# A two-layer transformer kernel: layer 0's opening in another order, and the stacked rows loaded in eight outer steps

## The reference, cut to what matters

```python
# layer 0: x is 8 x 512 x 128; c is 8 x 128
mod = (silu(c) @ wmod).reshape(8, 6, 1, 128)         # sa, ca, ga, sb, cb, gb; ga, gb kept >= 0.25 in size
h = layernorm(x) * (1 + ca) + sa
x = x + ga * attention0(h)
x = x + gb * top1_experts(layernorm(x) * (1 + cb) + sb)

def attention0(h):                                   # 16 heads of 8, 64 landmarks
    q_l, k_l = means of q, k over 8 neighbouring tokens
    L = softmax(q @ k_l.T); N = softmax(q_l @ k.T)
    K = softmax(q_l @ k_l.T)
    V = K.T / max(sum(K, axis=-2))
    for _ in range(6):
        KV = K @ V
        V = 0.25 * V @ (13 * I - KV @ (15 * I - KV @ (7 * I - KV)))
    return (L @ (V @ (N @ v))) @ W_proj

# layer 1, for each batch
scores = q @ k.T / sqrt(8) + bias[head, i - j]       # 16 heads, 512 tokens
bias[head, d] = sum over 21 of amp * exp(-|shp| * (d - off) ** 2)
# then a gated projection, causal attention over a latent, and 8 experts, two for each token
```

## Time and profile before

| | us |
|---|---|
| median of 3 runs (2076.03 to 2079.79) | 2079.36 |
| profiled execution, whole | 2073.5 |
| its span | 2071.5 |
| PE busy | 1779.4 (86%) |
| DVE busy | 1444.1 (70%) |
| ACT busy | 1015.6 (49%) |
| POOL busy | 857.9 (41%) |
| mean granted PE clock | 0.943 of full |

### The profile page before, as it was taken

How to read it: one execution, slowest core, us unless ns; L and a number is a source line. 1 busy time by engine, 2 the same in 40 slices (tenths; PEclk the granted TensorE clock), 3 DMA queues, 4 the chain that set the end, 5 groups by cost and what they waited for, 6 DMA issues and landing times.

```text
span 2071.5 us, 56863 instructions
## 1 busy us (share of the span) xinstructions
PE 1779.4 (86%) x21284; PEld 1306.9 (63%) x21284; DVE 1444.1 (70%) x4537; ACT 1015.6 (49%) x1992; POOL 857.9 (41%) x1253
## 2 busy tenths in 40 slices
PE   4485898898875729999999999999999999999997
PEld 2374677677763517766667666667666667766665
DVE  4574778876761127777787786787886887778765
ACT  1252544455441206666655654654654555655542
POOL 3500101110013017767655654655754663664530
PEclk7797999999996959999999999999999999999998
DMA  2512211222006411012013012012012112111211
GB/s 94 166 24 72 76 42 51 61 75 74 7 6 208 142 67 39 33 57 77 17 71 96 11 69 87 21 72 86 26 66 85 32 60 83 35 54 40 83 32 48
DMA packets 102694, 131.72 MB, mean 64 GB/s; under 512 B 14448, under 2 KB 87536, under 8 KB 101272
## 3 DMA queue, kind: packets, MB, share of 16 engines
q1 hardware_dynamic: 70600, 98.59, 14.6%
q10 hardware_dynamic: 28496, 18.10, 3.0%
q0 software_dynamic: 3328, 11.40, 1.7%
HBM read 100.05 MB, written 28.15 MB: 62 GB/s over the span
## 4 chain that ended last, share of the span: by engine, by line
PE 45%; DVE 8%; issue 6%; DMA 5%; POOL 2%; ACT 1%; ACTq 1%; SPq 1%; POOLq 0%; DVEq 0%
PE ps L1737 13%; PE ps L1752 7%; PE ps L1723 6%; PE ps L1846 5%; PE ps L1832 4%; DMA l_w_e<-in_L_ffn_w_dram 2%; DVE l_X L1900 2%; DMA l_stack<-parts_dram 2%; PE ps L1199 1%; POOL l_Y L1583 1%; PE ps L1208 1%; PE ps L1762 1%; PE ps L1783 1%; DVE l_xn L1931 1%; ACT PT L1625 1%
## 5 line engine op out<-in xcount | busy, mean ns | idle before, releaser
L1583 POOL TENSOR_SCALAR l_Y<-l_X,l_nmax 128x512 f32<-128x512 f32 (+3 forms) x1024 | 674.6, 664 | 521.1 <-PE ps L1737 286.0
L1625 ACT ACTIVATE PT<-ps 128x512 f32<-128x512 f32 (+3 forms) x1024 | 520.0, 517 | 405.8 <-PE ps L1737 356.3
L1737 PE MATMUL ps<-ident,l_Y 128*128 128x128 f32 x3328 | 549.7, 280 | 11.7 <-ACT PT L1625 7.7
L1737 PEld LDWEIGHTS ps<-ident,l_Y 128*128 128x128 f32 x3328 | 387.2, 142 | 195.3 <-issue 82.4
L1900 DVE CUSTOM_DVE_ANT_0 l_X<-ps,strips 128x512 f32<-128x512 f32 x512 | 342.1, 687 | 134.2 <-PE ps L1723 130.9
L1723 PE MATMUL ps<-l_stack 72*128 72x512 bf16 (+3 forms) x1024 | 351.0, 345 | 66.9 <-DVE l_nmax L1900 50.0
L1900 DVE CUSTOM_DVE_ANT_0 l_X<-ps,mask 128x384 f32<-128x384 f32 (+3 forms) x512 | 238.5, 485 | 41.0 <-PE ps L1723 35.6
L1752 PE MATMUL ps<-PT,v_aug 128*10 128x128 f32 x6656 | 230.1, 274 | 0.0
L1752 PEld LDWEIGHTS ps<-PT,v_aug 128*10 128x10 f32 x6656 | 156.8, 91 | 71.5 <-ACT PT L1625 42.6
L1723 PEld LDWEIGHTS ps<-l_stack 72*128 72x128 bf16 x1024 | 102.0, 100 | 102.6 <-DVE l_nmax L1900 77.3
L1832 PE MATMUL ps<-l_fT,l_w_e 128*128 128x512 f32 x256 | 138.9, 631 | 12.1 <-DMA l_w_e<-in_L_ffn_w_dram 9.3
(11 more groups left out here) (276 smaller groups left out, 2508.6 us busy)
## 6 DMA issues: line engine op xcount, KB each, us to landing
stack<-parts_dram SPq DMA_DIRECT2D x48, 384.0 KB
l_stack<-parts_dram SPq DMA_DIRECT2D x64, 288.0 KB
l_stack<-parts_dram SPq DMA_DIRECT2D x192, 96.0 KB
l_w_e<-in_L_ffn_w_dram ACTq DMA_DIRECT2D x128, 128.0 KB, 2.2
parts_dram<-l_parts SPq DMA_DIRECT2D x32, 384.0 KB, 2.5
strips<-bias_dram POOLq DMA_DIRECT2D x16, 448.0 KB, 11.2
parts_dram<-parts SPq DMA_DIRECT2D x16, 384.0 KB, 10.9
w_e<-in_L_ffn_w_dram SPq DMA_DIRECT2D x12, 256.0 KB, 5.7
```

Source lines behind the costliest of these rows:

```text
L1583: nc.gpsimd.tensor_scalar(Y[:, n % Y_BUFS, 0:w], X[:, n % X_BUFS, 0:w], -1.0, nmax[:, n % 8:n % 8 + 1], ALU.mult, ALU.add).then_inc(y_pool, 1)
L1625: nc.scalar.activation(dst, src, ACT.Exp).then_inc(moved, 1)
L1737: last = nc.tensor.transpose(ps[:, to, k * P:(k + 1) * P], Y[:, n % Y_BUFS, k * P:(k + 1) * P], ident[:])
```

## The change

- The fronts of batches 1 and 2 start at phases -8 and 1 (`front_at`) instead of -23 and -5. The others stay.
- The relative bias is computed in two halves of four slices. The exponents are VectorE's, at phases -37 and -27; ScalarE's exponentials stand at -32 and -26, GpSimd's scaling at -29 and -23, the sums at -21 and -20, and the two turns bT at -19 and -18 instead of 20 and 21.
- The halves are put together in one buffer and stored by one transfer, behind batch 0's stacks, x loads and modulation rows and before the zeros.
- The modulation is computed as columns on 128 partitions (twelve products instead of two narrow and two wide ones for each layer), worked on there, and turned once by TensorE. mods_dram and mod_row0 have their dimensions in another order.
- The marks and stacks of layer 0 come in three transfers for each of q and k, the source's outer step being the eight rows of a head and the inner one the three copies or parts (`spread`). So do those of each group in layer 1: six transfers instead of four. The order of the 72 rows changes alike for q and k.
- Waits of TensorE for w_proj, the router's weights and late constants move to where they are used.

```diff
-GAUSS_AT, REDUCE_AT, BIAS_AT, MODS_AT = -19, 2, PHASES + 2, -16
+EXPONENT_AT, SCALED_AT, REDUCE_AT, BIAS_AT, MODS_AT = (FRONT + 4, FRONT + 14), (FRONT + 12, FRONT + 18), FRONT + 20, FRONT + 22, FRONT + 10
...
+def front_at(b):
+
+    return {0: FRONT, 1: -8, 2: 1}.get(b, PHASES * b + FRONT)
...
-            [("xT", 0, FRONT + 4), ("q", 0, FRONT + 6), ("k", 0, FRONT + 6), ("v", 0, FRONT + 7)] +
+            [("xT", 0, 4), ("q", 0, 6), ("k", 0, 6), ("v", 0, 7)] +
...
+OF_CORE, OF_FRONT = ("Ks", "cs", "kT", "a0"), ("xT", "q", "k", "v")
...
+        def spread(sp, dst, dram, s, w, sem_):
+
+            for n in range(3):
+                src = [[H * w, HD], [0, 3] if s == 0 else [C * w, 3], [1, H * w]]
+                at = (3 * s + (n if s == 0 else 0)) * C * w
+                sp.dma_start(dst[3 * HD * n:3 * HD * (n + 1), s].rearrange("r h t -> r (h t)"),
+                             bass.AP(dram.tensor, at, src)).then_inc(sem_, 16)
...
-                def stack_q(b):
-
-                    sp.wait_ge(parts_stored[0], 16 * b + 16)
-                    flat = parts_dram[0].rearrange("n (d h) t -> (n d) (h t)", d=HD)
-                    for i in range(3):
-                        sp.dma_start(stack[b % 2][3 * HD * i:3 * HD * (i + 1), 0].rearrange("r h t -> r (h t)"),
-                                     flat).then_inc(stacked[0], 16)
-
-                def stack_k(b):
-
-                    sp.wait_ge(parts_stored[1], 16 * b + 16)
-                    for i in range(3):
-                        thrice = bass.AP(parts_dram.tensor, (3 + i) * C * T, [[0, 3], [H * T, HD], [1, H * T]])
-                        sp.dma_start(stack[b % 2][3 * HD * i:3 * HD * (i + 1), 1].rearrange("r h t -> r (h t)"),
-                                     thrice).then_inc(stacked[1], 16)
+                def stack_up(b, s):
+
+                    sp.wait_ge(parts_stored[s], 16 * b + 16)
+                    spread(sp, stack[b % 2], parts_dram, s, T, stacked[s])
...
+                        sp.wait_ge(bias_halves, 2)
+                        sp.dma_start(bias_dram, bias_hr).then_inc(bias_stored, 16)
...
-                    if b == 1:
-                        for k in range(2):
-                            sp.wait_ge(bias_half_ready, k + 1)
-                            sp.dma_start(bias_dram[:, k * T:(k + 1) * T], bias_hr[:]).then_inc(bias_stored, 16)
...
-                def exponent(n):
-                    if n == 0:
-                        pool.wait_ge(shp_ready, 1)
-                    gauss_chain.link(nc.gpsimd.tensor_scalar(dist[:, n % 2], off_[:], rel[:, n:n + 1], None, ALU.subtract))
-                    gauss_chain.link(nc.gpsimd.tensor_tensor(gauss[:, n], dist[:, n % 2], shp[:], ALU.mult))
-                    nc.gpsimd.tensor_tensor(gauss[:, n], gauss[:, n], dist[:, n % 2], ALU.mult).then_inc(exponent_ready, 1)
-
-                def scaled(n):
-                    pool.wait_ge(gauss_ready, n + 1)
-                    nc.gpsimd.tensor_tensor(gauss[:, n], gauss[:, n], amp[:], ALU.mult).then_inc(gauss_scaled, 1)
+                def scaled(half_):
+                    n = slice(4 * half_, 4 * half_ + 4)
+                    pool.wait_ge(gauss_ready, half_ + 1)
+                    nc.gpsimd.tensor_tensor(gauss[:, n], gauss[:, n], bc(amp[:].unsqueeze(1), [P, 4, H * KG]),
+                                            ALU.mult).then_inc(gauss_scaled, 1)
...
-                    for k in range(2):
-                        last = nc.tensor.matmul(ps[:, 0, (2 * l + k) * B:(2 * l + k + 1) * B],
+                    for k in range(6):
...
+                    if m == FRONT + 13:
+                        pe.wait_ge(mod_columns, 1)
+                        nc.tensor.transpose(ps[0:2 * 4 * B, 1, 0:P], modT[:].rearrange("p l k b -> p (l k b)"),
+                                            ident[:]).then_inc(mods_turned, 1)
...
+                def exponent(half_):
+                    part = slice(4 * half_, 4 * half_ + 4)
+                    wide_ = [P, REL // 2, H * KG]
+                    if half_ == 0:
+                        dve.wait_ge(gauss_loaded, 48)
+                        dve.wait_ge(consts_pool, 3)
+                        gauss_chain.link(nc.vector.tensor_copy(rel[:], rel_i[:]))
+                        gauss_chain.link(nc.vector.scalar_tensor_tensor(out=shp[:], in0=shp[:], scalar=-1.0, in1=shp[:],
+                                                                        op0=ALU.mult, op1=ALU.min))
+                    if half_:
+                        dve.wait_ge(exponent_ready, half_)
+                    gauss_chain.link(nc.vector.tensor_tensor(dist[:], bc(rel[:, part].unsqueeze(2), wide_),
+                                                             bc(off_[:].unsqueeze(1), wide_), ALU.subtract))
+                    gauss_chain.link(nc.vector.tensor_tensor(gauss[:, part], dist[:], bc(shp[:].unsqueeze(1), wide_), ALU.mult))
+                    nc.vector.tensor_tensor(gauss[:, part], gauss[:, part], dist[:], ALU.mult).then_inc(exponent_ready, 1)
+
+                def bias_sum(half_):
+                    part = slice(4 * half_, 4 * half_ + 4)
+                    dve.wait_ge(gauss_scaled, half_ + 1)
+                    nc.vector.tensor_reduce(bias_rel[:, part, :], gauss[:, part].rearrange("p n (h k) -> p n h k", k=KG), AX.X,
...
-                        front(b, off)
+                        front(b, m - front_at(b))
...
+                    for half_ in range(2):
+                        if m == EXPONENT_AT[half_]:
+                            exponent(half_)
+                        if m == REDUCE_AT + half_:
+                            bias_sum(half_)
...
-                    rows = [[0, 3], [H * T, 3 * HD], [1, 4 * T]]
-                    sp.dma_start(stack[0:9 * HD, 0, 4 * g:4 * (g + 1), :].rearrange("r h t -> r (h t)"),
-                                 bass.AP(parts_dram.tensor, g * 4 * T, rows)).then_inc(stacked[g], 16)
-                    for k in range(3):
-                        rows = [[0, 3], [H * T, HD], [1, 4 * T]]
-                        sp.dma_start(stack[3 * HD * k:3 * HD * (k + 1), 1, 4 * g:4 * (g + 1), :].rearrange("r h t -> r (h t)"),
-                                     bass.AP(parts_dram.tensor, (3 + k) * C * T + g * 4 * T, rows)).then_inc(stacked[g], 16)
+                    for k in range(2):
+                        for n in range(3):
+                            rows = [[H * T, HD], [0, 3] if k == 0 else [C * T, 3], [1, 4 * T]]
+                            at = (3 * k + (n if k == 0 else 0)) * C * T + g * 4 * T
+                            sp.dma_start(stack[3 * HD * n:3 * HD * (n + 1), k, 4 * g:4 * (g + 1), :].rearrange("r h t -> r (h t)"),
+                                         bass.AP(parts_dram.tensor, at, rows)).then_inc(stacked[g], 16)
```

More of the change, by code:

```diff
@@ L386, in mark @@
                     sp.wait_ge(marks_stored, 32 * (b + 1))
[L387 to L392 removed]
+                    for s in range(2):
+                        spread(sp, marks[b % 2], marks_dram, s, NL, marked)
                 def store(b, s):
@@ L553, in evacuate @@
                     if name == "bT":
-                        if k:
-                            act.wait_ge(bias_stored, 16)
-                        nc.scalar.copy(bias_hr[:], src[0:H]).then_inc(bias_half_ready, 1)
-                        act.wait_ge(bias_half_ready, k + 1)
-                        act.sem_inc(freed_act, 1)
+                        nc.scalar.copy(bias_hr[:, k * T:(k + 1) * T], src[0:H]).then_inc(freed_act, 1)
+                        wait_freed(act, NY_SLOT[what])
+                        act.sem_inc(bias_halves, 1)
                         return
@@ L590, in evacuate @@
                     if name == "LT":
-                        if b == 0 and k == 0:
-                            act.wait_ge(bias_rel_ready, REL)
+                        if b == 0 and k < 2:
+                            act.wait_ge((bias_rel_ready, bias_stored)[k], (2, 16)[k])
                         pairs = slice(4 * (k % 2), 4 * (k % 2) + 4)
@@ L997, in modulation @@
                         more(nc.vector.tensor_scalar_sub(sign[:], sign[:], 1.0))
-                        last = nc.vector.tensor_tensor(g, sign[:], size[:], ALU.mult)
-                        if k == 0:
-                            more(last)
-                    last.then_inc(mods_ready, 1)
-                def bias_sum(n):
-                    dve.wait_ge(gauss_scaled, n + 1)
-                    nc.vector.tensor_reduce(bias_rel[:, n, :], gauss[:, n].rearrange("p (h k) -> p h k", k=KG), AX.X,
+                        more(nc.vector.tensor_tensor(g, sign[:], size[:], ALU.mult))
@@ L1108, in _ @@
                         columns(0)
-                    if m == GAUSS_AT - 1:
-                        sharp()
+                    for half_ in range(2):
+                        if m == EXPONENT_AT[half_]:
+                            exponent(half_)
+                        if m == REDUCE_AT + half_:
```

(1 more changed line is left out.)

142 lines of the change are left out of this document (67 added, 75 removed).

## The result

| | before | after |
|---|---|---|
| median (range), us | 2077.7 (2071.4 to 2079.8), 4 runs | 2000.02 (1997.0 to 2002.2), 4 runs |
| ratio, 95% interval | | 0.9632 [0.9609, 0.9655] |
| profiled execution, us | 2073.5 | 2002.12 |
| its span, us; mean granted clock | 2071.5; 0.943 | 2000.4; 0.954 |

The kernel is 77.7 us faster by the medians. The forecast was 2017 us in 1992 to 2048, from 62.4 us won in the profile. So the time came out 9 us better in the profile, 17 by the medians.

What follows compares the result with a forecast made beforehand. TensorE was taken as nearly always busy in the second layer, so only its idle time could be won. The terms -21 + 3 - 23 - 13.4 - 6 - 2 gave -62.4 us, so 2017 us, range 1992 to 2048.

Steps and rivals of the forecast that it cites:

- Opening: First layer's start: first product of the iterations at 61 instead of 82.3 us, 21 us won, bounds 10 to 26.
- The price of wide operations: VectorE in the opening: 1.6 us for each operation of 1344 elements, the two bias sums 1.6 us each.
- the 58 to 64 named as a sign: Opening: TensorE's first X by AV_first at 58 to 64 us would show the forecast right.
- the front's products: Batch 1's front in the opening: TensorE's xT to v take 7.3 us at the half clock, ending at 61.0.
- Batch 0's iterations: First layer: batch 1's splits and batch 2's front now lie in them, 3 us lost, between 0 and 8.
- The stall in batch 1: First layer: SyncE no longer stands at the bias store, 23 us won, at least 19.8, at most 25.
- Layer 1, first stage: Second layer's first stage: gb_now lands sooner, y starts at 761.3 us, 13.4 us won, 8.7 to 15.
- Layer 1, the rest: Second layer's later stages: 6 us of expert weight waits and 2 of stack waits won, 0 to 12 for both.
- A: Rival: opening not won because VectorE has become its bound; 31 us won, 2049 us; chance 0.18.
- B: Rival: the spread does not come, three engines stay and only the order counts; 2065 us; chance 0.06.
- C: Rival: slower, SyncE bounds the second layer through dearer issues; 2125 us at 2.2 us an issue; chance 0.04.
- D: Rival: more won, as clock dips go too and batch 1 loses its bias turn; 80 won, 1999 us; chance 0.18.

Runs made afterwards that it cites:

- b_gauss8: Kernel before with GpSimd's eight bias slices started at phase -8 instead of -19, sums one phase later: 2072.97 us, ratio 1.0004.
- b_bias10: Kernel before with the bias's two turns at phases 10 and 11 instead of 20 and 21: 2046.25 us, ratio 0.9862.
- b_spread1: Kernel before with layer 1's stack loads alone in eight outer steps, six loads a group instead of four: 2044.02 us, ratio 0.9861.
- b_gauss8_spread0: Kernel before with bias slices from phase -8 and layer 0's stack and marks loads in eight outer steps: 2053.14 us, ratio 0.9901.
- a_front_old: Changed kernel with the fronts of batches 1 and 2 back at phases -23 and -5: 1996.62 us, ratio 0.9650.
- a_outer3: Changed kernel with stack and marks loads' two source steps swapped back in both layers; as built, part stayed single steps of 24 rows: 2024.49 us, ratio 0.9775.

## Why the prediction was right, and where its sizes were off

*Opening* (-21 forecast, -24.9). The mechanism is as told: rstd is no longer behind the slices. The price of wide operations was right (1.55 and 1.56 us against 1.6, the two sums 3.00 against 3.2). Two terms were too dear, so that the first product stood at 57.44, just ahead of the 58 to 64 named as a sign. AV_first ended at 43.99, not 46.5, since the marks' product, which I had left in its place, came two us earlier. Part of that comes from an edit to which I had given no price, the moved waits of TensorE. Batch 0's turn and its marks' product, before and then after:

```profile
10.72 1.09 PE L747 MATMUL ps<-ident,xn 128*128 128x128 f32 x4 [4.45 <-DMA w_router<-in_L_ffn_router_w_dram]
29.99 0.64 PE L759 MATMUL ps<-marks 72*64 72x64 bf16 x16 [9.54 <-DMA marks<-marks_dram]
```

```profile
9.32 1.09 PE L738 MATMUL ps<-ident,xn 128*128 128x128 f32 x4 [1.55 <-DVE xn L865]
27.93 0.64 PE L750 MATMUL ps<-marks 72*64 72x64 bf16 x16 [10.43 <-DMA marks<-marks_dram]
```

TensorE no longer stands for the router's weights, and 1.4 of the 2.1 us are there already at the turn. The rest of the miss, 0.7 us, is the front's products, which ran faster than at the half clock: v took 1.12 us instead of 1.71. What I had not priced is the companion. By b_gauss8 the earlier start alone is worth nothing in the end, because the store behind the triple loads lands 16.5 us later; I had used the shorter landing (7 us forecast, 9.5 measured) only to say that q's stack is there in time. The first product comes early without the spread. That the gain is still there at batch 1 needs it in the kernel before; in the changed kernel no run has the keys' loads in three steps.

*Batch 0's iterations* (+3, +0.7). Within the 0 to 8 given.

*The stall in batch 1* (-23, -24.9). Right in kind and size; b_bias10 has it alone, by nothing but an earlier place of bT and the bias store (25.4 us in batch 1, 24.6 up to the first expert turn).

*Layer 1, first stage* (-13.4, -12.8). Right: gb_now waits for 24 issues of 0.70 us on average (16.8 in all, 17.3 forecast) and lands in 3.8 (3 forecast). b_spread1 has it alone, 13.5.

*Layer 1, the rest* (-8, -9.3). Right in size: the weight waits went from 9.3 to 0.9 us (8.4 won, 6 forecast), and the slowest weight load from 9.5 to 5.5. The waits for the stack at later stages were 1.0 us in all and are gone, where 2 were forecast. b_spread1 has 9.7 alone.

*The rivals.* A (opening not won) and B (no spread) fall by the first product and by the share of 0.45 at 132 GB/s. C (dearer issues) falls by 0.70 us for one issue. D, 80 us won, came closest to the medians' 77.7, but its reasons are not shown. Batch 1 does win 1.9 us more than forecast. Its other reason, the clock, cannot be seen: TensorE's busy time fell from 1779.4 to 1773.1 us, and a second execution of the same loads has 1765.3. Of the 9 us by which the profile beats the sum, 3.9 are the opening, 2.3 batch 0, 1.9 batch 1 and 0.7 the rest, all within the bounds of each term. So the miss is the sum of small ones that lean the same way. The other 6 between profile and median are scatter.

Taken one at a time from before, the ratios are 0.9862 (bias store), 0.9861 (spread in layer 1) and 0.9901 (early start with spread in layer 0): 0.0138 + 0.0139 + 0.0099 = 0.0376, against 0.0368 for the whole change. That the sum fits so well is in part luck. The stall in batch 1 is in it more than once: b_bias10 takes all of it, and b_gauss8_spread0 takes 8 us of it again. On the other side the first product is at 68.64 in b_gauss8_spread0 and at 57.44 in after. By a_front_old (62.62) 5.2 of these 11.2 us are the fronts' places, of which little is left at the end. The other 6 are the bias pass on VectorE, the modulation as columns and the moved waits of TensorE, and none of these was tried by itself.

The Trainium skill's rule on engines for a transfer ("DMA: Bandwidth & Descriptors", section on why a DMA increments its semaphore by 16) gives eight of 16 for eight outer steps. The trace agrees: 0.45 of 16 is 7.2 engines from 694 to 712 us; that the loads were not always enough to fill eight is my reading. What no run here shows is a load of four steps.

## What to carry to other kernels

Ask of a transfer that reads rows several times in which order its steps stand: with the copies or parts outermost the share was 0.20 of 16, so about three DMA engines did the work, and what suffered was not the load itself but what was queued behind it (a store, a 64 KB row, the weights). An early start pays only if the buffers behind it come free as early, so look for the store that nobody waits for yet. And put a small load that an engine will wait for ahead of a block of issues, not behind it: here that was worth 11 us after the change and 17 before.

## What the runs showed of the hardware

- A store issued behind three loads of three outer steps landed after 16.5 us, behind the same loads in eight steps after 9.5 (b_gauss8 and b_gauss8_spread0).
- An issue of a stack load on SyncE took 0.65 to 0.73 us where the source has two steps above the rows, and about 0.37 where it has one (1.11 us for three of the keys' loads in a_outer3). Steps that fit into one stride were joined to one in the built loads: [C * T, 3], [H * T, 8] cost what 24 plain rows cost. Issues can be held: six loads of x took SyncE 5.17 us in before and 10.89 in after.
- Half of layer 1's loads in three outer steps cost more in weight waits (15.2 us) than all of them did before (9.3). Why is open; the loads then come closer together (24 issues in 14.1 us against 16 in 18.9), and a row behind them took 11.2 us to land, against 15 before and 3.8 after.
